# New hand-written instruction lists for the five engines of a four-layer graph network

## What is computed

```python
h = relu(_layernorm(x)); x = x + _L0_gnn_ref(h, adj, ...)   # 8 Euler steps of a graph diffusion
h = relu(_layernorm(x)); x = x + _L1_gnn_ref(h, adj, ...)   # graph attention: softmax_j(leaky(s1_i + s2_j)) Wh
h = relu(_layernorm(x)); x = x + _L2_gnn_ref(h, ...)        # attention over 256 edges src -> dst, 4 heads
h = relu(_layernorm(x)); x = x + _L3_gnn_ref(h, adj, adj, ...)
# _L3: h = relu(LN(L_norm @ x @ Wc + bc)); x1 = h + x
#      q, k, v = x1 @ Wq, x1 @ Wk, x1 @ Wv   (4 heads of 32)
#      scores = where(adj > 0, q k^T / sqrt(32), -1e9); o = softmax(scores) v
#      x2 = LN(x1 + o @ Wo + bo); y = LN(x2 + gelu(x2 @ W1 + b1) @ W2 + b2)
```

## Time and profile before

| | us |
|---|---|
| median of 3 runs | 1174.75 (1170.75 to 1177.1) |
| the profiled execution | 1172.26 |
| its span in the trace | 1170.5 |
| TensorE / VectorE / ScalarE / GpSimd busy | 1095.4 / 850.7 / 767.6 / 343.3 |
| granted TensorE clock, mean of the span | 0.979 |

### The profile page before, as it was taken

The page is one execution under the profiler, slowest core; times in us unless marked ns, Lnnn a source line. Parts: engine busy times, 40 slices in busy tenths (PEclk is TensorE's granted clock), DMA queues, the critical chain, the costliest instruction groups (busy, mean ns, idle before and its releaser), DMA issues. The chain is left out here.

```text
span 1170.5 us, 21096 instructions
## 1 busy us (share of the span) xinstructions
PE 1095.4 (94%) x7105; PEld 874.1 (75%) x7105; DVE 850.7 (73%) x3073; ACT 767.6 (66%) x1640; POOL 343.3 (29%) x465
## 2 busy tenths in 40 slices
PE   8999999999999977999999999999999999999785
PEld 5689899899898856777777777777777777766554
DVE  7864444354364477798898898898898898887665
ACT  4434534432232246898898898898898988987762
POOL 3312104103051012234325325235234244243123
PEclk9999999999999988999999999999999999999886
DMA  3002020021400112424334334334243243243421
GB/s 93 18 11 63 19 78 13 19 82 41 127 10 18 46 47 80 123 64 113 100 91 108 103 97 110 88 107 113 73 118 101 81 127 88 78 115 79 118 66 28
DMA packets 132940, 89.41 MB, mean 76 GB/s; under 512 B 13664, under 2 KB 115424, under 8 KB 132832
## 3 DMA queue, kind: packets, MB, share of 16 engines
q1 hardware_dynamic: 132768, 88.07, 27.7%
q0 software_dynamic: 64, 0.00, 0.0%
HBM read 33.50 MB, written 20.97 MB: 47 GB/s over the span
## 5 line engine op out<-in xcount | busy, mean ns | idle before, releaser
L2453 DVE CUSTOM_DVE_ANT_0 att_Ts<-bank,mask_att 128x512 f32<-128x512 f32 x256 | 174.4, 682 | 58.4 <-PE bank L2608 55.8
L2355 ACT ACTIVATE att_Es<-att_Ts,att_small 128x512 f32<-128x512 f32 x256 | 185.7, 725 | 31.3 <-DVE att_small L2453 31.0
L2662 PE MATMUL bank<-ident,att_Es 128*128 128x128 f32 x1024 | 159.3, 279 | 16.6 <-ACT att_PTs L2364 12.1
L2364 ACT COPY att_PTs<-bank 128x512 f32<-128x512 f32 x248 | 144.2, 581 | 45.9 <-PE bank L2662 44.7
L2662 PEld LDWEIGHTS bank<-ident,att_Es 128*128 128x128 f32 x1024 | 121.6, 143 | 54.8 <-ACT att_PTs L2364 25.8
L2608 PE MATMUL bank<-K_parts,Q_parts 128*128 128x512 f32 x256 | 125.1, 498 | 3.1 <-DMA K_parts<-k_lo 1.7
L2149 POOL TENSOR_SCALAR n_rs<-n_mv 128x4 f32<-128x4 f32 x46 | 15.4, 335 | 304.8 <-DVE n_mv L2144 304.8
L1593 PE MATMUL bank<-G_hi,UT_parts 128*128 128x384 f32 x288 | 77.3, 339 | 1.8 <-DVE G_lo L1436 1.8
L563 PE MATMUL bank<-gat_whs,gat_ETs 128*128 128x128 f32 x512 | 63.8, 280 | 2.0 <-PEq L149 2.0
L2608 PEld LDWEIGHTS bank<-K_parts,Q_parts 128*128 128x128 f32 x256 | 48.2, 193 | 22.3 <-issue 16.8
L563 PEld LDWEIGHTS bank<-gat_whs,gat_ETs 128*128 128x128 f32 x512 | 61.9, 196 | 2.4 <-issue 2.2
(11 more groups left out here) (350 smaller groups left out, 2908.2 us busy)
## 6 DMA issues: line engine op xcount, KB each, us to landing
Q_parts<-q_hi SPq DMA_DIRECT2D x128, 64.0 KB, 2.0
Q_parts<-q_lo SPq DMA_DIRECT2D x128, 64.0 KB, 2.0
K_parts<-k_hi SPq DMA_DIRECT2D x128, 64.0 KB, 2.0
K_parts<-k_lo SPq DMA_DIRECT2D x128, 64.0 KB, 2.0
l_x<-in_x SPq DMA_DIRECT2D x16, 256.0 KB, 2.9
gat_z<-x_after_l SPq DMA_DIRECT2D x16, 256.0 KB, 3.5
gat_xin<-x_after_l SPq DMA_DIRECT2D x16, 256.0 KB, 3.5
x_after_l<-x SPq DMA_DIRECT2D x16, 256.0 KB, 2.7
```

Of the source, the lines that this page charges most:

```text
L2355: nc.scalar.activation(att_E[:, j % RING_E, :], att_T[:, j % RING_T, :], ACT.Exp, scale=-1.0, bias=att_small[:, 0, j:j + 1], accum_out=att ...
L2364: nc.scalar.copy(att_PT[:, h, :, cols(q)], c2[:].rearrange("p (s q) -> p s q", q=P)).then_inc(sem("att_pt"), 1)
L2453: nc.vector.tensor_tensor_reduce(att_T[:, j % RING_T, :], [c0, c1][j % 2][:], k.mask_att[:, tile_of(n, j)[1], :], -QK_SCALE, HUGE, ALU.add ...
L2662: mm = nc.tensor.transpose(dst[:, cols(s)], att_E[:, i % RING_E, cols(s)], k.ident[:])
```

## The change

The three sets of lists (`ORDER`, `FILL_ORDER`, `DRAIN_ORDER`) are replaced for all five engines. The same steps are called for the same graphs, each once. `LAG` of `ffn` becomes 3, so a `+` is added to its steps, and the list of an iteration begins at another point of the round (at `att_turn12+` instead of `att_score0`); more steps carry `+` for that reason. `FILL` is the number 6, as before. Four waits that the old order made needless are written out: `gat_max0` and `gat_exp0` wait for the row terms in `gat_small`, every `att_mask` waits for the exp that frees its T tile, and every `att_score` for the mask that frees its bank; the last two were there for the last graph (and for scores 2 and 3). The diff, with the lists of the iteration whole and of fill and drain the lines that are spoken of:

```diff
@@ -444,6 +444,8 @@
                            ).then_inc(sem("gat_whs"), 1)
 
         def gat_exp(n, t):
+            if t == 0:
+                ready(act, "gat_small", n, 4, 4)
             ready(act, "gat_max", n, t + 1, NT)
             nc.scalar.activation(g.T[:, t, :], g.V[:, t, :], ACT.Exp, scale=0.8, bias=small[:, 4, t:t + 1],
                                  accum_out=small[:, 6, t:t + 1]).then_inc(sem("gat_exp"), 1)
@@ -498,6 +500,8 @@
             nc.vector.tensor_tensor(small[:, 4, :], wh1, small[:, 3, :], ALU.subtract).then_inc(sem("gat_small"), 1)
 
         def gat_max(n, t):
+            if t == 0:
+                ready(dve, "gat_small", n, 1, 4)
             nc.vector.scalar_tensor_tensor(g.V[:, t, :], a1[:], small[:, 5, t:t + 1], g.T[:, t, :], ALU.max, ALU.add
                                            ).then_inc(sem("gat_max"), 1)
 
@@ -1813,7 +1817,7 @@
 
 
 STAGES = ["gat", "edge", "cheb", "att", "ffn"]
-LAG = {s: i for i, s in enumerate(STAGES)}
+LAG = {"gat": 0, "edge": 1, "cheb": 2, "att": 3, "ffn": 3}
 TILES = H * NT
 RING_T, RING_E = 3, 4
 
@@ -1857,207 +1861,208 @@
 
 ORDER = {
     "PE": """
-        att_score0 att_score1 att_turn15+ att_rows+ att_pv0+ att_pv1+ att_score2 gat_turn att_turn0 att_score3 ffn_wo
-        cheb_prop0 att_turn1 att_score4 cheb_prop1 gat_wh cheb_g gat_s2 att_turn2 att_score5 ffn_turn att_turn3
-        ffn_up0 att_score6 ffn_up1 att_turn4 att_score7 ffn_down0 ffn_down1 cheb_x1turn att_turn5 att_score8
-        edge_gather0 att_turn6 edge_gather1 att_score9 cheb_q edge_x att_turn7 att_score10 gat_eturn0 edge_lcol
-        edge_lb0 edge_lb1 gat_eturn1 att_turn8 att_score11 cheb_k gat_eturn2 gat_eturn3 att_turn9 att_score12 edge_v
-        edge_den att_turn10 att_score13 gat_pv0 att_turn11 att_score14 edge_scatter att_turn12 att_score15 edge_out
-        att_turn13 gat_pv1 att_turn14 cheb_v
+        att_turn12+ att_score14+ att_score15+ edge_out+ att_turn13+ gat_pv1+ att_turn14+ att_score0 att_score1 cheb_v+
+        att_turn15+ att_rows+ att_pv0+ att_pv1+ att_score2 gat_turn att_turn0 att_score3 ffn_wo+ cheb_prop0 cheb_prop1
+        att_score4 gat_wh cheb_g att_turn1 att_score5 ffn_turn+ att_turn2 att_score6 gat_s2 ffn_up0+ ffn_up1+
+        att_turn3 att_score7 att_score8 ffn_down0+ att_turn4 ffn_down1+ cheb_x1turn att_turn5 edge_gather0
+        edge_gather1 att_score9 att_turn6 att_score10 edge_x cheb_q att_turn7 edge_lcol att_score11 gat_eturn0
+        att_turn8 edge_lb0 gat_eturn1 att_score12 edge_lb1 att_score13 cheb_k gat_eturn2 gat_eturn3 att_turn9 edge_v
+        edge_den att_turn10 gat_pv0 att_turn11 edge_scatter
     """.split(),
     "DVE": """
-        cheb_stats cheb_aggr gat_x2a+ att_rv+ gat_x2b+ gat_stats att_mask0 gat_aggr edge_stats att_mask1 edge_aggr
-        gat_apply cheb_lo att_scale att_mask2 att_mask3 ffn_y2 n2_stats n2_aggr att_mask4 n2_apply cheb_y n1_stats
-        att_mask5 gat_scores0 n1_aggr att_mask6 n1_apply att_mask7 cheb_x1 gat_scores1 gat_scores2 ffn_y3 gat_scores3
-        att_mask8 gat_row1 gat_row2 gat_row3 gat_max0 gat_max1 att_mask9 gat_max2 edge_z gat_max3 edge_lc att_mask10
-        cheb_qlow edge_max0 edge_max1 edge_max2 att_mask11 edge_max3 edge_le n3_stats att_mask12 edge_rden n3_aggr
-        edge_attn cheb_klow att_mask13 edge_u att_mask14 att_mask15 gat_rinv n3_apply edge_x3
+        edge_u+ n3_aggr++ gat_rinv+ cheb_klow+ n3_apply++ gat_stats att_mask14+ att_mask15+ edge_x3+ cheb_stats
+        cheb_aggr att_rv+ gat_aggr gat_x2a+ att_mask0 gat_x2b+ edge_stats att_mask1 gat_apply edge_aggr cheb_lo
+        att_scale+ att_mask2 att_mask3 ffn_y2+ n2_stats+ n2_aggr+ att_mask4 n2_apply+ cheb_y att_mask5 n1_stats
+        att_mask6 n1_aggr gat_scores0 n1_apply att_mask7 gat_scores1 cheb_x1 ffn_y3+ gat_scores2 gat_scores3 att_mask8
+        gat_row1 gat_row2 gat_max0 gat_row3 att_mask9 gat_max1 att_mask10 edge_z gat_max2 gat_max3 edge_lc att_mask11
+        cheb_qlow edge_max0 edge_max1 edge_max2 edge_max3 edge_le att_mask12 att_mask13 n3_stats+ edge_rden edge_attn
     """.split(),
     "ACT": """
-        cheb_apply cheb_hi att_exp0 att_exp1 gat_hT att_exp2 att_copy0 att_exp3 edge_apply cheb_xpT gat_wh_out0
-        att_copy1 gat_wh_out1 edge_hi att_exp4 att_copy2 ffn_x2T att_exp5 att_copy3 ffn_gelu0 ffn_gelu1 att_exp6
-        att_copy4 att_exp7 att_copy5 cheb_x1T att_exp8 att_copy6 edge_hg gat_exp0 cheb_qsplit edge_xz att_exp9
-        att_copy7 gat_exp1 gat_exp2 gat_exp3 gat_eT0 att_exp10 gat_eT1 att_copy8 att_exp11 edge_exp att_copy9 gat_eT2
-        gat_eT3 cheb_ksplit att_exp12 att_copy10 att_exp13 att_copy11 att_exp14 edge_yT att_copy12 att_exp15
-        att_copy13 att_copy14 att_copy15 cheb_vout att_spread
+        att_copy12+ att_exp14+ att_exp15+ att_copy13+ att_copy14+ att_copy15+ cheb_apply att_exp0 cheb_hi cheb_vout+
+        att_spread+ att_exp1 att_copy0 att_exp2 gat_hT att_exp3 edge_apply cheb_xpT gat_wh_out0 att_exp4 edge_hi
+        att_copy1 gat_wh_out1 ffn_x2T+ att_copy2 ffn_gelu0+ ffn_gelu1+ att_copy3 att_exp5 att_copy4 att_exp6 att_exp7
+        att_copy5 cheb_x1T att_exp8 edge_hg gat_exp0 att_copy6 edge_xz gat_exp1 att_copy7 cheb_qsplit att_exp9
+        gat_exp2 gat_eT0 gat_exp3 att_copy8 gat_eT1 att_exp10 gat_eT2 edge_exp att_copy9 gat_eT3 cheb_ksplit att_exp11
+        att_copy10 att_exp12 att_exp13 att_copy11 edge_yT
     """.split(),
     "POOL": """
-        cheb_rstd gat_rstd edge_rstd ffn_res n2_rstd edge_lo ffn_b2 n1_rstd n3_rstd ffn_x3b n3_g ffn_final
+        ffn_b2++ n1_rstd+ n3_rstd++ n3_g++ ffn_res+ ffn_x3b++ cheb_rstd gat_rstd ffn_final++ edge_rstd n2_rstd+
+        edge_lo
     """.split(),
     "SP": """
-        load_z load_x3+ stack0+ stack2+ store_out+ load_xr stack1+ stack3+ edge_store+ load_x store_v+ cheb_res load_v
+        load_z store_v++ stack3++ load_x3++ store_out+++ load_x+ cheb_res+ stack0+ load_v+ stack1+ edge_store+ stack2+
+        load_xr
     """.split(),
...
 FILL_ORDER = {
...
-        edge_out:1 gat_pv1:2 att_score2:0 cheb_v:0 att_turn0:0 att_score3:0 gat_turn:3 att_turn1:0 att_score4:0
...
-        gat_rinv:2 edge_attn:1 edge_u:1 att_mask0:0 att_mask1:0 edge_x3:1 cheb_stats:1 cheb_aggr:1 gat_x2a:2 gat_x2b:2
-        gat_stats:3 gat_aggr:3 att_mask2:0 gat_apply:3 edge_stats:2 edge_aggr:2 att_mask3:0 att_mask4:0 cheb_lo:1
...
+        edge_out:1 gat_pv0:2 gat_pv1:2 att_score2:0 att_turn0:0 att_score3:0 att_score4:0 gat_turn:3 att_turn1:0
...
+        cheb_stats:0 cheb_aggr:0 gat_stats:2 cheb_lo:0 gat_rinv:1 gat_x2a:1 gat_x2b:1 gat_aggr:2 edge_stats:1
+        gat_stats:3 edge_rden:1 edge_attn:1 edge_u:1 gat_aggr:3 att_mask0:0 att_mask1:0 edge_x3:1 cheb_stats:1
+        cheb_aggr:1 gat_apply:3 gat_x2a:2 gat_x2b:2 att_mask2:0 edge_stats:2 att_mask3:0 edge_aggr:2 att_mask4:0
...
+        cheb_apply:0 cheb_hi:0 cheb_xpT:0 edge_apply:1 gat_hT:2 gat_wh_out0:2 gat_wh_out1:2 edge_hi:1 edge_hg:1
...
+        cheb_rstd:0 gat_rstd:2 edge_rstd:1 n1_rstd:0 edge_lo:1 gat_rstd:3 cheb_rstd:1 edge_rstd:2 edge_lo:2 n1_rstd:1
+        load_z:2 load_z:3 cheb_res:0 edge_store:0 stack0:0 load_x:2 store_v:0 stack1:0 load_z:4 load_x:3 edge_store:1
...
 DRAIN_ORDER = {
...
-        att_turn12:15 att_score15:15 att_turn13:15 ffn_down0:14 ffn_down1:14 att_turn14:15 att_turn15:15 ffn_wo_0:15
...
-        ffn_gelu0:14 ffn_gelu1:14 att_exp13:15 att_exp14:15 att_copy12:15 att_exp15:15 att_copy14:15 att_spread_1:15
...
-        ffn_final:14 ffn_b2_0:15 n2_rstd_1:15 ffn_b2_1:15 n3_rstd_0:15 n3_rstd_1:15
...
+        att_score15:15 att_turn13:15 ffn_down0:14 ffn_down1:14 ffn_wo_0:15 att_turn14:15 att_rows_1:15 att_turn15:15
+        att_pv_1:15 ffn_turn_0:15 ffn_wo_1:15 ffn_up_0:15 ffn_down_0:15 ffn_turn_1:15 ffn_up_1:15 ffn_down_1:15
...
+        att_mask9:15 att_mask10:15 n2_apply:14 att_copy7:15 att_mask11:15 att_mask12:15 att_copy9:15 att_mask13:15
+        att_copy11:15 att_scale_0:15 att_mask14:15 att_mask15:15 att_copy13:15 ffn_y3:14 n3_stats:14 att_rv_1:15
+        n3_aggr:14 ffn_y2_0:15 n2_stats_0:15 n2_aggr_0:15 att_copy15:15 n2_gain_0:15 n2_apply_0:15 n3_apply:14
+        att_scale_1:15 ffn_y2_1:15 n2_stats_1:15 n2_aggr_1:15 n2_gain_1:15 n2_apply_1:15 ffn_y3_0:15 n3_stats_0:15
...
+        ffn_gelu0:14 ffn_gelu1:14 att_exp14:15 att_exp15:15 att_copy12:15 att_copy14:15 att_spread_1:15 ffn_x2T_0:15
...
+        n2_rstd:13 n1_rstd:15 ffn_res:14 ffn_x3b:13 ffn_b2:13 n3_rstd:13 n3_g:13 ffn_final:13 ffn_x3b:14 ffn_res:15
+        n2_rstd:14 ffn_b2:14 n3_rstd:14 n2_rstd_0:15 n3_g:14 ffn_final:14 n2_rstd_1:15 ffn_b2_0:15 ffn_b2_1:15
...
-FILL = 1 + max(LAG[STAGE_OF[step.rstrip("+")]] + step.count("+") for order in ORDER.values() for step in order)
+FILL = 6
 
 
 
@@ -2447,8 +2452,7 @@
                                         ).then_inc(sem(name + "_lo"), 1)
 
             def att_mask(n, j):
-                if last(n):
-                    need(dve, sem("att_exp"), n * TILES + j + 1 - RING_T)
+                need(dve, sem("att_exp"), n * TILES + j + 1 - RING_T)
```

(3 more changed lines are left out.)

265 lines of the change are left out of this document (127 added, 138 removed).

## The result

The changed kernel takes 1135.25 us (median, 1133.88 to 1136.56); the kernel before, beside it, 1173.41 (1170.75 to 1177.1). The ratio is 0.9668, 95% interval 0.9644 to 0.9692. The forecast was 1146.3 with a range of 1129 to 1172: the sign, the main term and the range held, and the gain was 38 us where 28 were forecast. The profiled execution took 1133.88, with a span of 1132.0 and a mean granted clock of 0.989.

A forecast was written before the change was run, and what follows sets the result against it. A pass was taken as bound by TensorE from `edge_x` round to `cheb_prop1`, then ScalarE to `edge_hg`. Passes -20.4, fill -4, drain -4 sum to -28.4: 1172.26 to 1143.9, median 2.5 above, 1146.3 us; range 1129 to 1172.

The forecast's parts named there:

- the main term: The twelve passes between fill and drain: 20.4 us less in all.
- The pass: One steady pass, 45.05 us before: hand-summed to 42.75, taken as 43.35, a gain of 1.7, bounds 42.2 and 45.3.
- Waits: Added semaphore waits on scores, masks, `gat_max` and `gat_exp`: cost taken as 0, at most 0.8 us a pass.
- rival (2): VectorE pays at the port lock each pass, `gat_apply` beside `ffn_final`: 11.6 us more, 1158 us; chance 0.12.
- SP's queue: Reordered stack transfers in the pass: value 0, bounds -0.3 and +0.5 us a pass.
- Fill: Stage before the twelve passes: shorter waits at `gat_turn:3` and `edge_lo:1`, -4 us, bounds -1 to -6.
- Drain: Stage after the twelve passes: two shorter TensorE waits, -4 us, bounds +2 and -9.
- The two waits it was built on: In the drain, `att_turn13:15` waiting 2.85 us and `ffn_wo_1:15` waiting 2.93: 1.8 and 1 to 2 back.
- Rival (1): ScalarE's stretch, `cheb_xpT` to `edge_hg`, keeps its length but for one copy: pass 44.6, total 1161 us; chance 0.15.
- (3): Nothing net: each stall moves to the next consumer, ends return their savings: 1169 to 1180 us; chance 0.10.
- (4): Slower: `att_turn5` waits for `att_exp5` and `att_copy4`, 1.2 us a pass, 1189 us; chance 0.07.
- (5): The floor of TensorE's work is nearly met: 41.9 us a pass, 1127 us; chance 0.06.

The follow-up runs named there:

- The last run: Changed kernel with `cheb_x1`, `att_mask8` earlier, `edge_hi` on GpSimd, `ffn_final` behind `edge_rstd`, 11 extra matmuls at the ends: 1144.11 us, ratio 0.9724 to the kernel before.
- The filled kernel: Kernel before plus 42 unread 256-column matmuls where TensorE waits in fill and drain, no step moved: ratio 0.9923, 9.0 us less.

## Why the prediction was right, and where it was off

*The pass: the term held.* 43.35 was taken, 43.17 measured; twelve passes gave -19.5 where -20.4 was forecast. That they agree so well is in part luck: a full pass gains 1.88 and not 1.7, but only ten of the twelve run under the new lists. `cheb_xpT` to `edge_x` is 13.66 (forecast 13.8), and the rest of the round 43.17 - 13.66 = 29.51 (forecast 28.95). `ffn_down0` waits less than forecast, and the new stalls forecast at `att_turn5` and `edge_x` are not there. One at `cheb_x1turn` is, which no step named, because VectorE's list was never added up. The number came out right with a chain missing that is as long as those in it. The hand sum itself was 42.75, and the 0.6 added to it for what such sums miss covered the 0.42 that it was short. By the prediction's prices TensorE's own work is 41.4 of the 43.17; its rows show 0.40 of the rest as a wait, and the other 1.4 are in pieces that aren't told apart.

*Waits:* 0 taken, 0.05 a pass measured.

*The lock at `gat_apply`, rival (2):* it is hit in the passes, 2.00 instead of 1.1, and costs nothing, for the reason given against it: `cheb_lo` behind it waits for ScalarE. The last run shows both halves, the lock off the path (0.88 saved, no gain) and on it (1.35 lost, 1.17 slower). `n3_apply` is at 1.11 as forecast, and its wait of 0.84 is a little over the 0.7 given as its bound.

*SP's queue:* no wait for a transfer in the pass.

*Fill: mis-sized.* -4 was taken with bounds of -1 and -6, and -9.0 measured. The wait at `gat_turn:3` went as forecast. Missed was the clock. Length times one minus the granted clock is 83.64 x 0.10 = 8.4 us before and 74.66 x 0.05 = 3.7 after. The filled kernel shows 2.6 of it to be time on the path with all waits still there. In the changed kernel TensorE's idle time in the fill falls from 13.4 to 8.9 us, 4.5, near the 4 that was taken for waits. Its busy time falls by as much, from 70.2 to 65.8: about 0.65 of that is work that went behind the stage's end (`cheb_v:1` out, `att_score2:1` in, by the prediction's prices), and the rest goes with a clock of 0.95 instead of 0.90.

*Drain: mis-sized most.* -4 was taken with bounds of +2 and -9, and -15.75 measured. The two waits it was built on give 3.3 alone. 3.7 come from the first piece, where the clock is 1.00 in both kernels: graph 13's pass with shorter company, which the prediction never costed. The clock, held up, gives 5.3 by itself. These can't simply be added: the 3.3, and 3.5 of the 5.3, lie in the same last piece, and no run has both. Another split goes by TensorE alone, which runs the same 752 matmuls in both drains: its idle time falls by 7.8 us, from 30.7 to 23.0, and its busy time by 8.0, from 109.8 to 101.8. The forecast's 4 stands against the 7.8, and the 8.0 had no term.

*What the prediction said of the clock* was only that it was 0.90 and 0.89 at the ends. It was read and not used: 140.50 x 0.11 = 15.5 us of the drain were there to be weighed, and a sum of waits leaves them out. Not all of such a figure comes back. Where two kernels have the same order and another clock, the length moved by about half of what it says: filled against before 2.6 of 5.1 in the fill and 5.3 of 11.4 in the drain, and 3.5 of 7.3 in the last two pieces of the new drain. The Trainium skill's "TensorE: Matmul & The Clock Gate", Part 1, says that the clock follows how busy TensorE has recently been; the filled kernel agrees, 0.97 instead of 0.89 in the drain.

*The errors by size,* against the profiled execution: passes +0.9, fill -5.0, drain -11.75, ahead of the fill +5.76. They sum to the 10.1 us by which the span fell more than the 28.4 forecast. The median lies 1.4 above the profiled execution where 2.5 was assumed. So the total is nearer than its parts: the ends were short by 16.7, and 5.8 of that is hidden by the stretch ahead of the fill, which has nothing to do with the change.

Rival (1) is near what the runs found, in another form: not ScalarE's stretch alone but chains of nearly equal length on three engines stop the pass at 43.17. Rivals (3), (4) and (5) did not come: the spacing is neither 45 nor 41.9, and `att_turn5` has no wait. The 1127 of (5) is 2 us too low by its own figures: 1174.75 - 12 x 3.15 - 8 = 1129.

## What to carry to other kernels

Before a stall is priced, add up every engine's list between the two events that close the round, the ones with no visible wait too: where three chains arrive together, removing any single wait or load gained nothing, and a delay added to one of them (0.29 at `att_mask8`) lengthened the pass by as much. Where the granted clock is under 1.00 and TensorE waits, a wait costs its length and the slower work behind it, so length times one minus the clock belongs in the range; about half of it came back here. A port collision is priced by what stands behind the slowed instruction: 0.88 us were free ahead of a wait, and 1.35 us cost 1.17 where the next step of TensorE's list waited for the result.

## What the runs showed of the hardware

The part ahead of the fill is the same code in all these kernels, and its length differed from execution to execution: the fill's first matmul starts between 404.7 and 412.7 us in fourteen traces. The clock goes with the difference. The kernel before and the changed one in the same stretches (windows), and what TensorE did ahead of the second drop:

```profile
30.00:38.00 8.00, 8.00 (x36) 5.50 (x37) 6.65 (x13) 3.10 (x8) 7.84 (x3) 1.00 0.12 33
267.00:275.00 8.00, 8.00 (x47) 8.00 (x47) 2.87 (x9) 0.62 (x1) 1.00 (x2) 1.00 0.00 0
```

```profile
34.00:38.00 4.00, 4.00 (x12) 2.02 (x11) 3.50 (x9) 0.33 (x1) 4.00 (x1) 0.70 0.00 0
...
267.00:271.00 4.00, 4.00 (x26) 4.00 (x26) 1.55 (x9) 1.83 (x5) 1.70 (x4) 0.69 0.00 0
271.00:275.00 4.00, 4.00 (x14) 4.00 (x13) 0.62 (x2) 0.00 (x0) 0.00 (x0) 0.50 0.00 0
```

```profile
265.88 4.44 PE L1664 MATMUL bank<-vec,asym 128*128 128x1 f32 x32
```

TensorE counts as fully busy throughout, but ahead of both drops it ran 32 matmuls of one column each (28.33 to 31.96 and 265.88 to 270.32). In the kernel before the same matmuls left the clock at 1.00. So the clock can fall behind a stretch that counts as busy without a gap, and with the same code the drop comes in some executions and not in others. All four traces that start the fill before 405 us are of the kernel before and versions of it, none of the six of the changed kernel and its versions; whether that is more than chance is open.
